# Preparation laid anew: the down and projection weights loaded behind the first stack, the scores of the preparation in pairs, one product a step, the second row normalised behind the third gated product

## The reference

```
xn = layernorm(x)                                  # (8, 512, 256)
q, k, v = split(xn @ qkv_w + qkv_b)                # 16 heads of 16
a = softmax(q k^T / 4) v ;  attn = a @ proj_w + proj_b
gate, up = xn @ (w_gate/127)^T, xn @ (w_up/127)^T  # int32 weights, 768 hidden
out = x + attn + (silu(gate) * up) @ (w_down/127)^T
```

## Time and profile before

| what | value |
|---|---|
| time, median of 3 runs | 587.43 us (584.62 to 587.61) |
| profiled execution, its own time | 585.34 us |
| its span in the profile | 583.5 us |
| PE matmul busy | 557.8 us, 96% |
| DVE busy | 466.9 us, 80% |
| ACT busy | 416.7 us, 71% |
| POOL busy | 303.9 us, 52% |
| preparation (to the first matmul of row 0) | 52.46 us |

### The profile page before, as it was taken

How to read it: one execution, slowest core, us unless ns; L and a number is a source line. 1 busy time by engine, 2 the same in 40 slices (tenths; PEclk the granted TensorE clock), 3 DMA queues, 4 the chain that set the end, 5 groups by cost and what they waited for, 6 DMA issues and landing times.

```text
span 583.5 us, 13815 instructions
## 1 busy us (share of the span) xinstructions
PE 557.8 (96%) x4844; PEld 335.0 (57%) x4844; DVE 466.9 (80%) x603; ACT 416.7 (71%) x572; POOL 303.9 (52%) x285
## 2 busy tenths in 40 slices
PE   8697799999999999999999999999999999998896
PEld 7455346555665556556665656555565657564453
DVE  5857579788878889788878889788889888788742
ACT  3725576788768886788758886688858886687663
POOL 3146443756467555756457555647457655255220
PEclk9989899999999999999999999999999999999999
DMA  8891438453773538552673638543673428630101
GB/s 277 211 249 22 110 127 217 76 123 62 206 202 66 129 127 232 93 126 56 196 199 66 137 107 237 108 116 60 193 195 67 113 97 241 120 56 17 60 2 37
DMA packets 55119, 74.89 MB, mean 128 GB/s; under 512 B 5680, under 2 KB 28208, under 8 KB 55088
## 3 DMA queue, kind: packets, MB, share of 16 engines
q1 hardware_dynamic: 55088, 74.47, 51.3%
HBM read 40.90 MB, written 33.03 MB: 127 GB/s over the span
## 4 chain that ended last, share of the span: by engine, by line
PE 88%; DMA 4%; DVE 3%; ACT 2%; issue 1%; SPq 1%; ACTq 0%; DVEq 0%
PE dense L1265 22%; PE o_bank L1239 21%; PE st_bank L1206 15%; PE dense L1309 14%; PE s_bank L1223 11%; PE dense L1249 2%; ACT probs L825 1%; DMA k_spread<-qk_parts 1%; DVE neg_max L986 1%; PE dense L1378 1%; DMA probs<-in_L_attn_qkv_w 1%; DMA xn_blocks<-x_turned 1%; DMA k_stack<-k_spread 1%; DMA x_turned<-xn 0%; PE st_bank L1223 0%
## 5 line engine op out<-in xcount | busy, mean ns | idle before, releaser
L986 DVE TENSOR_REDUCE neg_max<-s_bank 128x2 f32<-128x1024 f32 x250 | 304.9, 1219 | 75.2 <-PE s_bank L1223 73.9
L825 ACT ACTIVATE probs<-st_bank 128x1024 f32<-128x1024 f32 x250 | 256.4, 1026 | 114.8 <-PE st_bank L1206 111.7
L1239 PE MATMUL o_bank<-probs,v_ones 128*32 128x512 f32 x1024 | 137.2, 608 | 0.1
L1206 PE MATMUL st_bank<-q_stack,k_stack 50*128 50x512 f32 x500 | 118.3, 466 | 8.0 <-ACT probs L825 7.7
L1206 PEld LDWEIGHTS st_bank<-q_stack,k_stack 50*128 50x128 f32 x500 | 47.9, 185 | 134.6 <-ACT probs L825 84.9
L1223 PE MATMUL s_bank<-k_stack,q_stack 48*128 48x512 f32 x500 | 109.0, 429 | 4.9 <-DMA k_stack<-k_spread 3.0
L732 POOL TENSOR_TENSOR hid_tl<-gated,hid_th 128x512 fp32r<-128x512 f32 x48 | 61.7, 1285 | 36.2 <-ACT hid_th L925 36.2
L726 POOL TENSOR_TENSOR gated<-gated,hid 128x512 f32<-128x512 f32 x48 | 61.7, 1285 | 35.7 <-DVE gated L1008 22.2
L1265 PE MATMUL dense<-xn_tl,w_uh 64*128 64x512 f32 x176 | 61.9, 392 | 0.0
L1265 PE MATMUL dense<-xn_tl,w_gh 64*128 64x512 f32 x176 | 61.9, 391 | 0.0
L1223 PEld LDWEIGHTS s_bank<-k_stack,q_stack 48*128 48x128 f32 x500 | 47.4, 185 | 24.4 <-DVE neg_max L986 9.3
(11 more groups left out here) (152 smaller groups left out, 890.8 us busy)
## 6 DMA issues: line engine op xcount, KB each, us to landing
q_stack<-q_spread SPq DMA_DIRECT2D x64, 192.0 KB, 4.7
k_stack<-k_spread SPq DMA_DIRECT2D x64, 192.0 KB, 5.2
q_spread<-qk_parts SPq DMA_DIRECT2D x16, 512.0 KB, 4.6
k_spread<-qk_parts SPq DMA_DIRECT2D x16, 512.0 KB, 3.6
q_spread<-qk_parts SPq DMA_DIRECT2D x16, 256.0 KB, 4.5
k_spread<-qk_parts SPq DMA_DIRECT2D x16, 256.0 KB, 2.1
resid<-in_L_attn_x SPq DMA_DIRECT2D x16, 256.0 KB, 3.8
out<-resid SPq DMA_DIRECT2D x15, 256.0 KB, 2.2
```

The lines of the kernel that those rows point to most:

```text
L825: nc.scalar.activation(probs[:, s % 2, 2 * half:2 * half + 2, :], transposed_bank(row, s, half)[:, :, :], ACT.Exp, scale=SCALE).then_inc(e ...
L986: nc.vector.tensor_reduce(neg_max[:, g % 2, :, NT * pair + qt], score_bank(row, half)[:, :, :], AX_X, ALU.max, negate=True).then_inc(max_d ...
L1206: done = nc.tensor.matmul(transposed_bank(row, s, half)[:, r, :], k_stack[rows, pair, P * kt:P * (kt + 1)], q_stack[rows, pair, :], start= ...
L1239: done = nc.tensor.matmul(o_bank[32 * j:32 * (j + 1), :], v_ones[:, kt, 8 * (g // 2) + 2 * j + g % 2, :], probs[:, (s - 1) % 2, j, :], sta ...
```

## The change

The table of the preparation is laid out anew. q 1 and k 1 move ahead (steps 4, 5), up 0 is made ahead of the first scores, and after that each step has one product of the feed-forward layer, in slot 2, behind both of the step's scores; the three `wdown` chunks move from step 4 to steps 12 and 13. The loads of `w_down`, `proj_w` and of the two biases that hang on them are issued behind the load of stack 0 instead of behind `w_up`. `w_down` is made float by ACT, behind gate 1 (DVE before); the low part of `proj_w` is made by POOL at step 12 (DVE before), where the spread of v's bias now is also. The normalisation of row 1 keeps its place, (13, 2), but up 3 now comes later, so that POOL normalises behind the third gated product and not behind the fourth. The squares move with the chunks that they follow. The rows after the preparation keep their tables.

```diff
-    (4, 0, "wdown", 0, 1), (4, 0, "wdown", 1, 1), (4, 0, "wdown", 2, 1),
-    (5, 0, "q", 1, 1), (6, 0, "k", 1, 1),
-    (7, 0, "gate", 0, 1),
-    (10, 1, "up", 0, 1), (10, 2, "gate", 1, 1),
-    (11, 1, "up", 1, 1), (11, 2, "gate", 2, 1),
-    (12, 1, "up", 2, 1), (12, 2, "gate", 3, 1),
-    (13, 1, "up", 3, 1), (14, 1, "max", 0, 1), (15, 1, "v", 0, 1),
+    (4, 0, "q", 1, 1), (5, 0, "k", 1, 1),
+    (7, 0, "gate", 0, 1), (8, 0, "up", 0, 1),
+    (10, 2, "gate", 1, 1),
+    (11, 2, "up", 1, 1),
+    (12, 1, "wdown", 0, 1), (12, 1, "wdown", 1, 1), (12, 2, "gate", 2, 1),
+    (13, 1, "wdown", 2, 1), (13, 2, "up", 2, 1),
+    (14, 1, "max", 0, 1), (14, 2, "gate", 3, 1),
+    (15, 1, "v", 0, 1), (15, 2, "up", 3, 1),
...
-SQUARES_AFTER = (("wdown", 2), ("k", 1), ("max", 0))
+SQUARES_AFTER = (("k", 1), ("up", 0), ("wdown", 2))
+PROJ_LOW_AT = (12, 0)
...
+            def load_later_weights():
+                raw_weight(4, raw_d.bitcast(I32).rearrange("p (k n) -> p k n", n=HID),
+                           w_down.rearrange("(k p) n -> p k n", p=P))
+                raw_weight(1, raw_p, proj_w.rearrange("(k p) n -> p k n", p=P))
+                sp.dma_start(v_bias[:, :], qkv_b[2 * C:3 * C].rearrange("(k p) -> p k", p=P),
+                             allow_slow_non_contiguous=True).then_inc(v_bias_in, 16)
+                sp.dma_start(p_bias[:, :], proj_b.partition_broadcast(P)).then_inc(bias_in, 16)
...
                 if row.has(1):
                     heads_spread(row, 0)
                     load_stack(row, 0)
+                if row.like == -1:
+                    load_later_weights()
...
+                        if row.like == -1 and (s, slot) == PROJ_LOW_AT:
+                            pool.wait_ge(v_bias_in, 16)
+                            nc.gpsimd.tensor_copy(v_bias_rows[:, :, :], v_bias[:, :].unsqueeze(2).broadcast_to([P, KC, P])
+                                                  ).then_inc(v_bias_wide, 1)
+                            pool.wait_ge(w_high, 3)
+                            nc.gpsimd.tensor_tensor(w_p[1][:, :, :], raw_p, w_p[0][:, :, :].bitcast(F32),
+                                                    ALU.subtract).then_inc(w_p_low, 1)
...
-                            if row.like == -1 and chunk[2:4] == ("wdown", 2):
+                            if row.like == -1 and chunk[2:4] == ("gate", 1):
+                                act.wait_ge(w_in[4], 16)
+                                nc.scalar.activation(raw_d, raw_d.bitcast(I32), ACT.Copy).then_inc(w_down_float, 1)
                                 split_high_of_weights(1, w_p[0][:, :, :], raw_p)
...
-                elif after == ("wgate", 2):
-                    to_float(4, raw_d)
                 elif after == ("wdown", 2):
-                    split_low(3, w_p[1][:, :, :], raw_p, w_p[0][:, :, :])
```

More of the change, by code:

```diff
@@ L352, in build @@
         w_float = sem("w_float")
+        w_down_float = sem("w_down_float")
+        w_p_low = sem("w_p_low")
         squares_done = sem("squares_done")
@@ L571, in spread_heads @@
                              qk_parts[i][:, which, 1 - HIGH_AT[which], :].bitcast(F32)).then_inc(spread[i], 16)
+            def load_later_weights():
[5 more added lines that the diff above has]
+                sp.dma_start(p_bias[:, :], proj_b.partition_broadcast(P)).then_inc(bias_in, 16)
             def heads_spread(row, i):
-                sp.wait_ge(bias_in, 16)
+                if row.like >= 0:
+                    sp.wait_ge(bias_in, 16)
                 sp.wait_ge(spread[i], 16 * SPREADS * (row.at + 2))
@@ L626, in step @@
                                w_up.rearrange("(k p) n -> p k n", p=P))
[L627 to L632, removed]
                 if row.like == 0:
@@ L774, in step @@
                     deviation(0)
-                    pool.wait_ge(v_bias_in, 16)
-                    nc.gpsimd.tensor_copy(v_bias_rows[:, :, :], v_bias[:, :].unsqueeze(2).broadcast_to([P, KC, P])
-                                          ).then_inc(v_bias_wide, 1)
                     pool.wait_ge(dense_done, count(row, any_chunk, kind="wup", index=2))
@@ L1354, in chunk_before @@
                 if kind == "wdown":
-                    pe.wait_ge(w_float, 3)
+                    pe.wait_ge(w_down_float, 1)
                     d = raw_d.rearrange("p (k n) -> p k n", n=HID)
```

## The result

The changed kernel takes 578.22 us (median of 4 runs, 577.52 to 579.84) against 586.02 us of the kernel before (4 runs, 582.94 to 587.61): a ratio of 0.9868, 95% interval 0.9824 to 0.9912. That is 7.7 us saved, between 5.2 and 10.3, where 4.0 was forecast. In a second set it took 579.44 us (6 runs) against 585.89 (29 runs), ratio 0.9897 (0.9846 to 0.9947). The profiled execution took 579.84 us, its span is 578.0 against 583.5 before: 5.5 us less.

A forecast was written before the change was run, and what follows sets the result against it. PE was taken to bound the loop's rows (65.92 of 66.00 us), so only row 0's start counted. Stack 3.5 plus stretch 0.5 made 4.0 us, giving 581.3 or 583.4 by base; forecast 582.5 us, range 579.8 to 586.3.

The forecast's parts named there:

- The steps up to the first score: Preparation: four products ahead of the scores, up 0 done at 25.2 to 25.6, PE waiting about 1 us, stack at 26.3.
- Row 0 begins at 48.4, 22.1 us behind the stack: End of the preparation: a walk of the new order gave 48.0, plus 0.4; before, row 0 began at 52.46.
- stretch 0.5: Term of the sum: from stack 0's landing to row 0's start, 22.1 us instead of 22.6, 0.5 us saved.
- the hand-offs that I had added on top: Stretch from stack to row 0: 0.4 us added to the walk's 48.0 for hand-offs of 0.1 to 0.3 us.
- The base of the forecast: Starting time of the whole kernel: between the profiled execution's 585.34 and the runs' median of 587.43 us.
- A: Rival, chance 0.18: half clock behind the shorter wait, or w_down landing late, leaves a gain of 1.5 to 3 us.
- B: Rival, chance 0.12: k's write is late from its own parts, not bytes ahead of it; gain 0 to 1 us.
- C: Rival, chance 0.07: moved loads reach ACT late, w_down at 33.7 us; gain gone or slower, up to 590 us.
- Costs put at nothing: Work moved to ACT and POOL, row 1's normalisation place and row 0's shifted stall: each claimed to cost 0 us.
- Nothing here to win: Row 0's stall, where PE stands 3.5 us for the turned row 1: claimed only to shift with row 0.
- the stack's best case (4.6 us): Upper end of the gain: stack 0 landing 4.6 us earlier, where the forecast took 3.5.
- my walk's floor (21.7 us): Upper end of the gain: stretch from stack 0 to row 0 of 21.7 us, where the forecast took 22.1.

The follow-up runs named there:

- before_turn: The kernel before with DVE's two turnings of row 1 moved from row 0's step 0 to the end of the preparation; 581.70 us, ratio 0.9951.
- again: The changed kernel once more, unaltered, beside the kernel before on the same chip; 579.44 us, ratio 0.9897.
- max_first: The changed kernel with the two small loads of group 0's maxima issued ahead of stack 3's load in the preparation; 579.74 us, ratio 0.9897.
- busy_row0: The changed kernel with 30 transposes of the identity put on PE in row 0's stall; 579.75 us, ratio 0.9901.
- turn_early: The changed kernel with DVE's two turnings of row 1 moved from row 0's step 0 to the end of the preparation; 574.66 us, ratio 0.983.
- turn_max: turn_early with the small loads of the maxima also ahead of stack 3, as in max_first; 574.19 us, ratio 0.9818 to the kernel before.
- norm_fourth: The changed kernel with row 1's averages and normalisation moved from (13, 2) to (15, 2), behind the fourth gated product; 583.66 us, ratio 0.9959.
- up0_late: The changed kernel with up 0 between the first two scores again and the squares of w_up's low part behind gate 0; 581.93 us, ratio 0.9933.
- loads_early: The changed kernel with the loads of w_down, proj_w and the two biases issued right behind w_up again; 583.96 us, ratio 0.997.
- before_again2: The kernel before, unaltered, the second of three more profiles of it; 587.78 us.

## Why the prediction was wrong, point by point

**The direction and the mechanism were right.** The steps up to the first score came out as worked out: the four products ahead, up 0 done at 25.2, PE waiting about 1 us (1.15), the stack at 26.3 (26.34). Undoing the loads gives 4.5 us back. In the profiles of one set it is 3.5 us of the stack (29.04 against 25.57) and 0.9 of the stretch behind it (21.62 against 20.71 us), in which the clock is at half again.

**"Row 0 begins at 48.4, 22.1 us behind the stack" is the step that failed.** It began 20.98 us behind it, 20.7 in the other profiles of the changed order (46.28 less 25.57). The term of the sum that it gave, stretch 0.5, measured 1.7 us. The mis-sized part is DVE's: 12 reductions and 12 other instructions taken at their durations, one behind the other. Back to back they overlap by some 0.09 us each. From its first reduction at 26.88 to its last one's end at 46.24 DVE took 19.36 us, 0.88 of them idle, so it was busy for 18.48 us with what I had summed to 19.6 (my terms add up to 19.7). Its eighth reduction ended at 39.54 and not at 40.5. The rows of before would have told it:

```profile
48.85 1.20 DVE L986 TENSOR_REDUCE neg_max<-st_bank 128x2 f32<-128x1024 f32 x1
49.98 1.20 DVE L986 TENSOR_REDUCE neg_max<-s_bank 128x2 f32<-128x1024 f32 x1
```

They start 1.13 us apart. Stack 1, which I had on time, gave some 0.2 us of it back: it landed 12.0 us after its last issue (27.46 to 39.5), not by about 38, and DVE idled 0.22 us there. The tenth score, from which PE runs on to row 0, stood at 40.14 and not 40.8; from there to row 0 it took 7.2 us, as I had it. So 0.7 us of the 1.1 are DVE's overlap, and 0.4 are the hand-offs that I had added on top.

**The gain was also sized on one profile of the kernel before.** The base of the forecast was right: 582.5 and 4.0 make 586.5 us, and 586.02 was measured. But I took one profile as the kernel before. Its preparation takes 49.4 to 55.5 us, according to how late the stack is and how often the clock falls. Over all profiles of the two orders (five of before with before_turn, six of the changed one with again, max_first, busy_row0, turn_early and turn_max) the first score moves from 29.5 to 25.8 us in the mean and the stretch behind it from 22.9 to 20.8. That is 3.7 us for the stack, where I had 3.5, and 2.1 for the stretch, where I had 0.5. Their sum of 5.8 us lies by the 6.0 of the second set and inside the interval of the first (5.2 to 10.3); that the first came out at 7.7 isn't explained further. Of 93 timed executions of it the time falls from 591.3 us at a mean granted clock of 0.980 to about 583.1 at 0.994 (correlation -0.96; a line through them has 0.49 us for each 0.001). The changed kernel's ten executions have 0.991 to 0.997 and 577.5 to 581.4 us. The means are 585.9 at 0.9885 and 579.1 at 0.9947. By the line 0.0062 of clock is 3.1 us of the 6.8 between them, and the rest 3.7 is there at equal clock. This is a reckoning along a line, no experiment that holds the clock alone. A late stack lengthens the wait and lowers the clock together, so the 3.1 us are not shown to be the clock's; the kernels with PE kept busy, which tried to hold it alone, can't tell a us or two.

**The rivals.** A: the clock didn't fall behind a wait of 1.15 us, nor of 1.69 in norm_fourth; it fell after 2.06 (before_turn) and after 2.8 us and more. That it would hold after 1 us was a guess that no row spoke for, as the prediction says. So the section of the Trainium skill that I weighed ("TensorE: Matmul & The Clock Gate", "HAM oscillation — how this bites in real kernels") speaks for the change: the shorter wait keeps the clock. up0_late and loads_early show the other side, with waits of 3.07 and 3.65 us and clocks of 0.62 and 0.64 over the 4 us behind them. B was refuted by loads_early. C: `w_down` landed 7.0 us after its issue at 21.38, at 28.4, ACT began with it at 29.20 without waiting.

**Costs put at nothing.** The normalisation's place gains nothing, and its cover is real: 4.2 us without it. Row 0's stall shifted with row 0. In the second profile it kept its length (PE 3.62 us, 3.55 before). In the first it was 4.28 us: the first transposed score waited for the maxima, behind stack 3 in the queue, and SP took 2.70 us and not 1.84 to issue the turn's DMAs. "Nothing here to win" holds for this change only: turn_early took most of the stall away, and 4.8 us with it.

**The range** ended at 579.8 and the result is 578.2. Its lower end was made from one profile's 585.34 with the stack's best case (4.6 us) and my walk's floor (21.7 us). It held nothing for a stretch below the walk (20.7 to 21.0 was measured), nor for the kernel before differing from one execution to the next.

## What to carry to other kernels

A load that nobody needs yet costs what stands behind it in the queue: move it behind the first one that is waited for, and fill the engines with what needs neither. Take from the timeline how far apart the starts of back-to-back instructions are, not how long one lasts, before you sum an engine that bounds a stretch. And look at more than one profile of the kernel before: where a wait makes the clock fall, what a change saves differs from execution to execution, and a change that shortens the wait also takes away the spread.

## What the hardware showed that was not expected

- Waits of 0.4 to 1.15 us ahead of the first score left the clock at 1.00, also that of 1.69; 2.06, 2.84, 2.86, 3.01, 3.07 and 3.65 us were each followed by half clock (0.50 to 0.64 over the next 4 us), down to 1.2 GHz. In row 0 a wait of 1.83 us was followed by it too (before_turn), one of 0.88 not (turn_early). A single wait is not all: in before_again2 the clock fell again near 50 us, behind waits of 0.81 and 0.61 us, where the same two waits in the first profile of before left it at 1.00. Transposes of the identity in the wait held it at 1.00 (25 in 2.89 us, 50 in 5.6), whereas the Trainium skill ("TensorE: Matmul & The Clock Gate", Part 4, PE-mode transpose) says that they don't count as busy in the same way. Here the measurement decides, with one reserve: the trace lists the transposes as MATMUL and doesn't show whether they ran in that mode.
- A transpose of 128 columns of float took 112 ns (5.6 us for 50) at full clock.
- The first score, which waits for stack 0, stood between 28.2 and 30.4 us in the kernel before and between 25.1 and 27.4 with the loads moved. This alone moves the time by 2 us.
